# The attention's order of matmuls: planned by a list scheduler instead of paced by a formula

## The reference

```
att = einsum('bhql,bhkl->bhqk', q_for_k, k_lat) * L ** -0.5
att = where(causal, att, -inf)
att = softmax(att, axis=-1)
y_lat = einsum('bhqk,bhkl->bhql', att, v_lat)
```

## Time and profile before

| | us |
|---|---|
| median of 3 runs | 3211.87 (3208.84 to 3214.44) |
| profiled execution | 3208.24 |
| its span | 3206.6 |
| TensorE busy in the span | 2898.4 (90%) |
| VectorE busy | 2264.1 (71%) |
| ScalarE busy | 1904.9 (59%) |
| GpSimd busy | 777.2 (24%) |
| attention: first matmul starts, last turning starts (span's clock) | 465.8, 2340.0 |

### The profile page before, as it was taken

The page is one execution under the profiler, slowest core; times in us unless marked ns, Lnnn a source line. Parts: engine busy times, 40 slices in busy tenths (PEclk is TensorE's granted clock), DMA queues, the critical chain, the costliest instruction groups (busy, mean ns, idle before and its releaser), DMA issues. The chain is left out here.

```text
span 3206.6 us, 50279 instructions
## 1 busy us (share of the span) xinstructions
PE 2898.4 (90%) x16538; PEld 1928.7 (60%) x16538; DVE 2264.1 (71%) x5659; ACT 1904.9 (59%) x3718; POOL 777.2 (24%) x700
## 2 busy tenths in 40 slices
PE   7888858999999999999999999999969998699990
PEld 6676744555555555555555555555447776699990
DVE  7999966877878877787888778788424544455444
ACT  4666623666666666666666666666735444465544
POOL 5777840010000001000000110100014454232320
PEclk9999976999999999999999999999979999899995
DMA  4666682242143234224314322431073221343316
GB/s 153 220 229 219 216 241 61 51 100 66 35 100 75 47 79 97 53 51 100 75 30 97 81 69 51 100 73 28 8 257 126 96 79 36 81 102 96 77 21 216
DMA packets 259647, 320.07 MB, mean 100 GB/s; under 512 B 70578, under 2 KB 157787, under 8 KB 258144
## 3 DMA queue, kind: packets, MB, share of 16 engines
q1 hardware_dynamic: 241760, 294.09, 32.3%
q0 software_dynamic: 17664, 23.19, 3.8%
HBM read 182.76 MB, written 143.95 MB: 102 GB/s over the span
## 5 line engine op out<-in xcount | busy, mean ns | idle before, releaser
L692 ACT ACTIVATE att_probs<-att_score_bank 128x512 f32<-128x512 f32 (+3 forms) x2560 | 1194.8, 540 | 654.2 <-PE att_score_bank L634 638.6
L725 DVE TENSOR_REDUCE att_partial_max<-att_max_bank 128x1 f32<-128x512 f32 x1536 | 1001.1, 683 | 164.0 <-PE att_max_bank L622 160.3
L622 PE MATMUL att_max_bank<-att_k_st,att_q_st 96*128 96x512 f32 (+3 forms) x2560 | 979.0, 406 | 72.2 <-DVE att_partial_max L725 40.5
L634 PE MATMUL att_score_bank<-att_q_st,att_k_st 98*128 98x512 f32 (+3 forms) x2560 | 927.7, 379 | 10.5 <-DMA att_q_st<-att_max_rows 5.0
L622 PEld LDWEIGHTS att_max_bank<-att_k_st,att_q_st 96*128 96x128 f32 x2560 | 481.3, 192 | 451.4 <-DVE att_partial_max L725 263.1
L729 DVE CUSTOM_DVE_ANT_0 att_edge_sum<-att_max_bank,att_edge 128x128 f32<-128x128 f32 (+3 forms) x1024 | 480.9, 482 | 182.0 <-PE att_max_bank L622 180.9
L711 POOL TENSOR_SCALAR_AFFINE_SELECT att_probs<-att_probs 128x512 f32<-128x512 f32 x256 | 163.0, 637 | 1710.1 <-ACT att_probs L692 1710.1
L634 PEld LDWEIGHTS att_score_bank<-att_q_st,att_k_st 98*128 98x128 f32 x2560 | 486.0, 191 | 148.3 <-ACT att_probs L692 68.6
L648 PE MATMUL att_acc_bank<-att_probs,att_v_st 128*32 128x512 f32 (+3 forms) x5120 | 541.9, 541 | 0.6 <-ACT att_probs L692 0.4
L648 PEld LDWEIGHTS att_acc_bank<-att_probs,att_v_st 128*32 128x32 f32 x5120 | 135.7, 110 | 261.6 <-ACT att_probs L692 132.1
L210 POOL TENSOR_TENSOR proj_op_low<-proj_turned,proj_op_high 128x512 fp32r<-128x512 f32 x192 | 274.9, 1462 | 58.7 <-ACT proj_op_high L332 58.5
(11 more groups left out here) (220 smaller groups left out, 3872.0 us busy)
## 6 DMA issues: line engine op xcount, KB each, us to landing
qk_parts<-proj_parts SPq DMA_DIRECT2D x64, 1024.0 KB, 4.5
att_q_st<-qk_parts SPq DMA_DIRECT2D x192, 256.0 KB, 4.4
att_k_st<-qk_parts SPq DMA_DIRECT2D x192, 256.0 KB, 6.4
v_tokens<-proj_v_tok SPq DMA_DIRECT2D x64, 256.0 KB, 4.4
att_v_st<-v_tokens SPq DMA_DIRECT2D x64, 256.0 KB, 7.0
exp_w<-in_ew SPq DMA_DIRECT2D x16, 1024.0 KB, 8.8
dispatched<-mix_empty_rows SPq DMA_DIRECT2D x8, 1036.0 KB, 14.3
exp_rows<-dispatched SPq DMA_DIRECT2D x16, 518.0 KB, 5.2
```

What stands on the lines that cost most here:

```text
L622: nc.tensor.matmul(max_ps[u % MAXB][:, 0:width], q_st[0:3 * L, n % QBUF, j, t * P:(t + 1) * P], k_st[0:3 * L, g % 2, kb, j, 0:width], star ...
L634: nc.tensor.matmul(score_ps[h % SCOREB][:, q0:CH], k_st[:, g % 2, kt // TT, j, (kt % TT) * P:(kt % TT + 1) * P], q_st[:, n % QBUF, j, q0:C ...
L692: nc.scalar.activation(probs[:, k % PROBS, j, q0:CH], score_ps[(HG * k + j) % SCOREB][:, q0:CH], ACT.Exp).then_inc(exped, 1)
L725: nc.vector.tensor_reduce(best, bank[:], AX.X, ALU.max).then_inc(unit_reduced, 1)
```

## The change

The formula and its constants go. A class `Order` walks through the attention once when the program is built. It keeps a modelled clock for TensorE, VectorE, ScalarE, GpSimd and SyncE's queue, and at each point lists what TensorE could issue next (the next unit, score, weighing or turning) with the modelled time at which its inputs and its bank are there. It picks by a price: the waiting time, plus a tenth of the backlog of the engine that would receive the result; a weighing pays more when fewer than two steps are ready (`GATHER`), or while VectorE or ScalarE has little left to do. After one weighing a second is joined if it is ready within 0.1 us (`JOIN`), at most two in a burst (`BURST`). The picks are kept as counts (`units_before_score` and so on), and `attend` issues the same instructions in that order.

Counted from the rules: TensorE has 2560 units, 2560 scores, 640 weighings and 64 turnings in both orders. Before, the weighings lie in 320 bursts of two; after, in 289 of two and 62 of one. 48 units stood ahead of the first score, and 36 do now. In the middle slots a turning follows its chunk's last weighing by six or seven instructions before and by three or four after.

Other edits: VectorE divides once the units that TensorE issues ahead of the turning are reduced; ScalarE copies `acc` behind the last exponential whose score stands ahead of the last weighing, as before, now by the new counts; SyncE's shift rows and stores follow the new counts; GpSimd fills the rows of ones of the first of the two key buffers, waits for it, and fills the second when it reaches the second chunk; TensorE waits for the first fill ahead of the first score, not ahead of the first unit, and for the second ahead of the first score of the second slot; `acc` is one tile instead of a list of one.

```
@@ -426,21 +426,32 @@
 MU = [(s, c, j, t, kb) for s in range(SLOTS) for c in range(NC) for j in range(HG) for t in range(TT) for kb in range(c + 1)]
 NK, NS, NU = len(KS), HG * len(KS), len(MU)
 CHUNKS = SLOTS * NC
-PAIR = 2
-ACCS = 1
-MAXB = 4
-SCOREB = 3
+BURST = 2
+GATHER = 2
+EVEN = 0.1
+JOIN = 0.1
+MAXB, SCOREB = 4, 3
 PROBS = 3
 QBUF = 6
-AHEAD = 3
-TURN_AFTER = 3
-MARGIN = 20
-FIRST_UNITS = 24
-DIVIDE_BACK = 2
+STORE_AFTER = 6
 
 
 def chunk_of(s, c):
     return s * NC + c
+def unit_columns(u):
+    s, c, j, t, kb = MU[u]
+    return CH if kb < c else (t + 1) * P
+def first_query(k):
+    s, c, kt = KS[k]
+    return max(kt - TT * c, 0) * P
+def on_diagonal(u):
+    return MU[u][4] == MU[u][1]
 
 
 FIRST_STEP = [KS.index((n // NC, n % NC, 0)) for n in range(CHUNKS)]
@@ -448,39 +459,140 @@
 UNITS_THROUGH = [1 + max(u for u in range(NU) if chunk_of(*MU[u][:2]) == n) for n in range(CHUNKS)]
 
 
-def pace_maxima():
-
...
-MAXIMA_BEFORE = pace_maxima()
+class Order:
+    MODE, DRAIN = 0.112, 0.17
+    def __init__(self):
+        self.units_before_score = [0] * NS
+        self.scores_before_weighing = [0] * NK
+        self.units_before_weighing = [0] * NK
+        self.scores_before_turn = [0] * CHUNKS
+        self.units_before_turn = [0] * CHUNKS
+        self.weighed_before_turn = [0] * CHUNKS
+        self.now, self.tiled, self.burst = 0.0, False, 0
+        self.u = self.h = self.w = self.turned = 0
+        self.vector = self.scalar = self.pool = self.queue = 0.0
+        self.reduced, self.exped, self.weighed = [0.0] * NU, [0.0] * NS, [0.0] * NK
+        self.masked, self.read, self.divided = {}, {}, {}
+        self.rows, self.parts_due = {}, []
+        while self.h < NS or self.w < NK or self.turned < CHUNKS:
+            self.step()
+    def starts(self):
+        free, tiled = self.now + self.MODE * self.tiled, self.now + self.MODE * (not self.tiled)
+        at = {}
+        u, h, w = self.u, self.h, self.w
+        if u < NU and chunk_of(*MU[u][:2]) - chunk_of(*KS[min(h, NS - 1) // HG][:2]) <= QBUF - 2:
+            at["unit"] = max(free, self.reduced[u - MAXB] if u >= MAXB else 0.0)
+        if h < NS and h // HG - PROBS < w:
+            s, c, kt = KS[h // HG]
+            first = h % HG == 0 and kt == 0
+            if not first or chunk_of(s, c) in self.rows:
+                at["score"] = max(free, self.exped[h - SCOREB] if h >= SCOREB else 0.0,
+                                  self.rows[chunk_of(s, c)] if first else 0.0)
+        if w < NK and HG * (w + 1) <= h:
+            s, c, kt = KS[w]
+            n = chunk_of(s, c)
+            if kt or n == 0 or n - 1 in self.divided:
+                at["weigh"] = max(tiled, self.exped[HG * w + HG - 1], self.masked.get(w, 0.0),
+                                  self.divided[n - 1] if kt == 0 and n else 0.0)
+        if self.turned in self.read:
+            at["turn"] = max(free, self.read[self.turned])
+        return at
+    def step(self):
+        at = self.starts()
+        backlog = {"unit": max(self.vector - self.now, 0.0), "score": max(self.scalar - self.now, 0.0)}
+        if self.tiled and "weigh" in at and self.burst < BURST and at["weigh"] - self.now <= JOIN:
+            pick = "weigh"
+        elif not self.tiled and "turn" in at and at["turn"] <= self.now + 0.05:
+            pick = "turn"
+        else:
+            price = {}
+            for kind, start in at.items():
+                price[kind] = start - self.now
+                if kind in backlog:
+                    price[kind] += EVEN * backlog[kind]
+                if kind == "weigh":
+                    k = self.w
+                    while k < NK and HG * (k + 1) <= self.h and self.exped[HG * k + HG - 1] <= self.now + 0.9 * (k - self.w) + 0.3:
+                        k += 1
+                    few = k - self.w < GATHER and self.w + GATHER < NK
+                    price[kind] += 0.5 * few + 0.3 * max(0.0, 1.1 - backlog["unit"]) + 0.3 * max(0.0, 1.0 - backlog["score"])
+                if kind == "turn":
+                    price[kind] -= 0.1
+            pick = min(price, key=price.get)
+        start = at[pick]
+        if pick == "weigh":
+            self.weigh(start)
+        elif pick == "unit":
+            self.unit(start)
+        elif pick == "score":
+            self.score(start)
+        else:
+            self.turn(start)
+    def weigh(self, start):
+        k = self.w
+        self.scores_before_weighing[k], self.units_before_weighing[k] = self.h, self.u
+        self.burst = self.burst + 1 if self.tiled else 1
+        self.tiled = True
+        self.now = start + (CH - first_query(k)) / 600 + 0.03
+        self.weighed[k] = self.now + self.DRAIN
+        n = chunk_of(*KS[k][:2])
+        if k + 1 == LAST_STEP[n]:
+            self.scalar = max(self.scalar, self.weighed[k]) + 0.49
+            self.read[n] = self.scalar + 0.16
+        self.w += 1
+    def unit(self, start):
+        u, columns = self.u, unit_columns(self.u)
+        self.tiled = False
+        self.now = start + columns / 2400 + 0.02
+        ready = self.now + self.DRAIN + 0.02
+        wait = 0.13 if on_diagonal(u) and ready > self.vector else 0.0
+        self.vector = max(self.vector, ready) + wait + columns / 960 + 0.07
+        self.reduced[u] = self.vector + 0.135
+        n = chunk_of(*MU[u][:2])
+        if u + 1 == UNITS_THROUGH[n]:
+            self.vector += 0.2
+            self.parts_due = [(u + 1, 0.17), (u + 2, 0.27), (u + 3, 0.2)]
+        while self.parts_due and (u >= self.parts_due[0][0] or u + 1 == NU):
+            self.vector += self.parts_due.pop(0)[1]
+            if not self.parts_due:
+                self.queue = max(self.queue, self.vector + 0.1) + 5.0
+                self.rows[UNITS_THROUGH.index(u + 1) if u + 1 == NU else n - 1] = self.queue + 2.0
+        self.u += 1
+    def score(self, start):
+        h, k = self.h, self.h // HG
+        columns = CH - first_query(k)
+        self.units_before_score[h] = self.u
+        self.tiled = False
+        self.now = start + columns / 2400 + 0.02
+        slot_free = self.weighed[k - PROBS] if k >= PROBS else 0.0
+        self.scalar = max(self.scalar, self.now + self.DRAIN + 0.04, slot_free) + columns / 1400 + 0.12
+        self.exped[h] = self.scalar + 0.16
+        s, c, kt = KS[k]
+        if h % HG == HG - 1 and kt >= TT * c:
+            self.pool = max(self.pool, self.exped[h] + 0.1) + 0.64
+            self.masked[k] = self.pool + 0.05
+        self.h += 1
+    def turn(self, start):
+        n = self.turned
+        self.scores_before_turn[n], self.units_before_turn[n], self.weighed_before_turn[n] = self.h, self.u, self.w
+        self.tiled = False
+        self.now = start + 0.5
+        self.vector = max(self.vector, self.now + self.DRAIN) + 0.68
+        self.divided[n] = self.vector + 0.13
+        self.turned += 1
+ORDER = Order()
 
 
...
-        acc = [ps(f"acc{i}", [P, CH]) for i in range(ACCS)]
+        acc = ps("acc", [P, CH])
 
...
-        def weigh_after(n):
-
-            return min(HG * LAST_STEP[n] + AHEAD, NS) - 1
-
-        def turn_after(n):
-
-            return min(weigh_after(n) + TURN_AFTER, NS - 1)
-
-        def turned_at(h):
-
-            ends = [n for n in range(CHUNKS) if turn_after(n) == h and weigh_after(n) < NS - 1]
-            return ends[0] if ends else None
-
-        def divide_after(n):
-
-            units = MAXIMA_BEFORE[turn_after(n)]
-            return units - DIVIDE_BACK if units < NU else NU + 4
+        def read_after(n):
+            return ORDER.scores_before_weighing[LAST_STEP[n] - 1] - 1
 
         @block.sync
         def _(sp):
@@ -592,10 +690,10 @@
             put_next = store_next = 0
             load_next = NC
             for h in range(NS):
-                while put_next < CHUNKS and MAXIMA_BEFORE[h] >= min(UNITS_THROUGH[put_next] + 2, NU):
+                while put_next < CHUNKS and ORDER.units_before_score[h] >= min(UNITS_THROUGH[put_next] + 2, NU):
                     put_shift(put_next)
                     put_next += 1
-                while store_next < CHUNKS and turn_after(store_next) + 6 <= h:
+                while store_next < CHUNKS and ORDER.scores_before_turn[store_next] + STORE_AFTER <= h:
                     store_y(store_next)
                     store_next += 1
                 g, c = divmod(load_next, NC)
...
             pe.wait_ge(consts_in, 32)
-            pe.wait_ge(ones_set, 1)
-            u = weighed = 0
-            for h in range(NS):
-                while u < MAXIMA_BEFORE[h]:
-                    max_unit(u)
-                    u += 1
-                score(h)
-                while weighed < NK and h == min(HG * PAIR * (weighed // PAIR + 1) + AHEAD, NS) - 1:
-                    weigh(weighed)
-                    weighed += 1
-                n = turned_at(h)
-                if n is not None:
-                    turn_sums(n)
-            turn_sums(CHUNKS - 1)
+            u = weighed = turned = 0
```

(38 more changed lines are left out.)

38 lines of the change are left out of this document (6 added, 32 removed).

## The result

The changed kernel took 3116.12 us (median of 4 runs, 3112.8 to 3118.34), against 3211.85 before: the ratio is 0.9697, 95% interval 0.9685 to 0.9709. That is 96 us less, where 116 were forecast. The profiled execution took 3112.8, its span is 3111.2.

The account below looks back on a forecast made before the run. TensorE bounds the kernel, with 14.0 of a slot's 112.9 us waits from poor order. Net 7.4 us a slot over 15 slots (111) and 5 in the head take 3208.2 to 3092, forecast as a 3096 us median, range 3040 to 3175.

Parts of the forecast that it names:

- forecast case: Whole kernel: the main outcome, 3065 to 3155 us, given a chance of 0.61.
- sum of spacings: TensorE's slot if it never waited, from undisturbed start distances: 98.9 us of 112.9, the other 14.0 being waits.
- Term b: Chunk change: VectorE divides two units later, no longer idle before scored units; 2.5 us a slot back, bounds 0 and 3.2.
- Term a: Weighings on TensorE: 351 bursts instead of 320, each of the 31 more costing 0.23 us; 0.5 us a slot lost.
- Term c: Waits outside the chunk changes, 10.8 us a slot: the planned order takes half, 5.4 us.
- good cycle: Full tiles where the old order alternates well, 1534.02 to 1539.85: 5.58 us by spacings, 5.83 taken, so 4% stays.
- The sign that was to show this term: Over 14 slots, units' waits on VectorE were to be about half of the 223 us.
- Term d: Head: earlier units and a filled 5.01 us wait, against a lower clock; 5 us gained, bounds 20 lost and 20 gained.
- the 1.8 us where it would decide: Rival, chunk changes: the turning blocks TensorE, 2.1 us in each of 64, 3230 us, deciding from 1.8 us; chance 0.07.
- nearly waitless case: Rival, slots: only the forced 1 us and 3 us of late starts stay, 9 to 10 us a slot, 3045 to 3065; chance 0.12.

Follow-up runs that it names:

- e3_before_divide_late: The kernel before with DIVIDE_BACK 0 instead of 2, so VectorE divides after the units that TensorE issues ahead of the turning; 3165.8 us, ratio 0.9852.
- e12_before_single: The kernel before with DIVIDE_BACK 0 and PAIR 1, every step weighed in a burst of its own, 640 bursts instead of 320; 3358.7 us, ratio 1.0458.
- e4_pairs_only: The changed kernel with the planner allowed to weigh only pairs of steps, 320 bursts of two and no single ones; 3157.9 us, ratio 0.9839.
- e6_half_reduce: The changed kernel, order untouched, with VectorE reducing only the first 256 of each full unit's 512 columns; 3104.6 us, ratio 0.9667.

## Why the prediction was right, and where its sizes were off

**The sum.** 7.4 us a slot were forecast and 6.3 came; the head was to give 5. In all 116 forecast, 96 measured, inside the forecast case's own range. The sign, the place and the main causes were right. The starting point was 0.5 us a slot too low: counting turnings made 1580 us into fourteen slots and 112.9 us each, but a slot takes 113.4, so 14.5 us stood above the sum of spacings and not 14.0.

**Term b, the chunk change.** Forecast 2.5 us a slot. e3_before_divide_late measured 2.7 by itself, and 3.8 with the new order around it. This one line of VectorE's order is about half of the change's gain.

**Term a, more bursts.** Forecast 0.5 us a slot at 0.23 us a burst. A burst costs 0.1 more than that, since the first matmul behind it starts late (1514.34 above), which is 0.6 us a slot. That single bursts cost more by what they wait for was shown by e12_before_single only for the old, fixed distance of three scores. In the planned order single bursts pay for themselves: without them, e4_pairs_only, a slot is 1.6 us longer.

**Term c, the rest of the order, is the step that was mis-sized.** Forecast 5.4 us a slot, "half" of 10.8. Measured: from e3_before_divide_late to the changed kernel 3.6, and 4.2 with term a's 0.6 put back. The 10.8 were not all waits. The late start behind 20 bursts and 4 turnings, 2.4 us a slot, belongs to the sum of spacings and had been counted as a wait; of the 8.4 that remain, 8.9 with the slot put right, the change took 4.2, about the half that was assumed. The timelines say the same directly: between units and scores 8.6 us a slot stand above the spacings in e3_before_divide_late and 4.1 in the changed kernel. That the share was half had no row behind it, so that part was a lucky guess. The prediction had the late start in its own good cycle: 0.1 of the 0.25 us that it read as "even a good cycle leaves 4%" is the one behind the burst.

The sign that was to show this term, units' idle weight loads on VectorE at about half of 223 us, went further, to 74, while the time gained was less than forecast. The list of waits does not tell how much of a wait is path.

**Term d, the head.** Forecast 5 us gained. The head and the first slot gave 7.3 together, but that contains the first slot's share of the better order. The 3 us of earlier units came and were worth at most 0.9, since the first score waits for its row. The second half of the fill was called hidden beside chunk 1's steps, with "one mask late" as the worst; the trace shows it stopping VectorE for 6.56 us and TensorE for 5.77. The prediction looked for who waits for GpSimd, and not for who shares something with it.

**The rivals.** The turning does wait for ScalarE's copy, in three of four cases, but most of that lies under the running matmul: it costs about 0.1 us a turning, far from the 1.8 us where it would decide. No slot came down by the 9 to 10 us of the nearly waitless case.

**What stays open:** what makes the many steps of 0.02 to 0.12 us between units and scores, 3.7 us a slot together. With VectorE's or ScalarE's full work halved the 4.1 us fall only to 4.0 and 3.4. Both halved at once was not tried.

## What to carry to other kernels

Before pricing a planner's new order, look at where the engines that follow it place their own work: here one in-order engine stood at a wait two items too early, and moving that alone was worth half of the whole rearrangement. When waits are estimated as the difference between a measured period and a sum of spacings, read the spacing behind every kind of switch too, or fixed costs pass for waits. And a filler put "beside" other work on an idle engine needs a look at what that engine shares with the busy ones.

## What the runs showed of the hardware that was not expected

- A VectorE cast of 16 columns took 6.56 us while GpSimd filled memory for 6.92 us, and ended with it; 0.16 us without. In e6_half_reduce, which keeps the split fill, the same cast took 6.87 us and ended with the fill again.
- The first matmul behind a burst of four-tile matmuls keeps its successor 0.34 us instead of 0.234, and behind transposes 0.32 (changed kernel, medians of 307 and 56 cases: 0.103 and 0.080 us more).
- In the middle of dense work (e4_pairs_only) a stretch of 4.5 us in which TensorE issued only ten units and a turning was followed by 10.2 us at the clock's lower level, with TensorE busy throughout. Six of seven such stretches were followed by a fall, of 3.4 to 10.2 us, and one was not. In e12_before_single a fall of 10.2 us came behind 7 us in which TensorE had stood idle three times, for 0.84, 0.51 and 0.85 us.
